# L1-distance attention of a fused vision tower: one score tile in sixteen moves from VectorE to ScalarE and TensorE

## The chip, the cores and the metric

The kernel runs on one core of a Trainium2 chip. The metric is the device time of one execution in microseconds (us), lower is better. The core has a matrix engine (TensorE, PE in the profile), a vector engine (VectorE, DVE), a scalar engine (ScalarE, ACT), a general engine (GpSimd, POOL) and a queue engine that issues most transfers (SyncE, SP). Each runs its own instruction list in order, and they meet at semaphores. SBUF is the working memory; PSUM, which TensorE writes, has eight banks of 512 f32 columns on 128 partitions, called `ps[0]` to `ps[7]` here.

## The reference

The program is a small vision tower: wavelet tokens, linear attention, a mixture of experts, an L1-distance attention, and a routed MLP, each on a layernorm of the stream `h` of 128 images, 64 tokens each, 64 wide. The change lies in the L1-distance attention, whose core is this:

```python
def one_query(qs):
    return -jnp.sum(jnp.abs(qs[:, None, :, :] - k), axis=-1) * scale
...
a = jnp.concatenate([a, jnp.zeros((b, 1, t, h), a.dtype)], axis=1)
a = jax.nn.softmax(a, axis=1)[:, :t]
bf = jnp.einsum('bsdh,bshw->bdhw', a, vf)
bb = jnp.einsum('bdsh,bshw->bdhw', a, vb)
o = (bf + bb).sum(axis=2).reshape(b, t, d)
y = o * jax.nn.sigmoid(1.702 * o)
y = y @ fanin_w.T + fanin_b
```

For every image, each of 64 x 64 pairs of tokens and each of 8 heads needs the sum of 64 absolute differences: 2,097,152 differences an image, or 16 tiles of 128 partitions x 1024.

## The kernel before

Images are worked on in 64 pairs (`pair`, one body in each engine's program; pairs 4 to 63 run in a hardware loop of two pairs a turn). Within a pair, image `b` = 0 comes first, then `b` = 1. In each image TensorE makes the 16 difference tiles in the order of the string `ORDER` (line 36, function `image`): position `k` in 0 to 15 is a letter. A tile is two f16 matmuls of 512 columns that pick a query row and subtract the keys (both sit as high and low f16 halves in `blocks`).

- **D tiles** (11 an image, line 760) alternate between banks 0/1 and 2/3. VectorE turns each into 16 columns of `score` by one reduction with absolute value over 128x1024 (`reduce`, line 1364). TensorE may write D tile d only when reduction d-2 is done.
- **A tiles** (5 an image, line 754) go one half each to banks 4 and 5. ScalarE takes the absolute value of each half into `absd0` or `absd1` (`absolute`, line 1004), and may be at most one tile behind. GpSimd sums the five tiles of an image in a tree of additions (`batch`, lines 1473 and 1477), and starts when all of them are there.

Between tiles, at written-out positions `k`, the function `extra` inside TensorE's `pair` hangs the rest of the attention:

```python
if k == 10:
    queries(q + 1, at)
if k == 12:
    low(q + 1, 1 - odd, 0)
if k == 14:
    keys(q + 1, 1 - odd)
```

`queries` (669) and `keys` (673) form the projections of the next pair in bank 6. ScalarE writes their high halves to `qk` as f16 (`high_q` 978, `high_k` 982). `low` then makes the same f32 product a second time (681 or 679) and subtracts the high half by one f16 matmul (682), and ScalarE stores what is left (986). SP copies `qk` into `blocks` (`fill_blocks`, 389). Other extras are `values_b` (689), `values_f` (696), the transpose of the inputs (`turn`, 663), the transposes of the attention (`turn_attn`, 704), its products with the values (`attend`, 720 and 725, in three parts), the transpose and projection of the gated result (`turn_y` 731, `fan_in` 735). Bank 7 is shared by `turn`, `attend`, `turn_y` and `fan_in`. When the scores of an image are done, SP spreads them into `attn` (`spread`, 8 transfers an image, 398). ScalarE takes eight exponentials of the previous pair, four after position 10 of image 1 and four after position 13 (`exponentials`, 1016). VectorE has three small steps a pair besides: `reciprocals` (1349), `finish` (1359) and `gated` (1354); GpSimd one, `normalise` (1484).

## Time and profile before

| | |
|---|---|
| runs, us | 2650.24, 2652.99, 2647.89 (median 2650.24) |
| profiled execution, us | 2650.77 |
| its span, us | 2648.9 |
| share of the span busy | PE 85%, DVE 85%, POOL 66%, ACT 56% |
| first score reduction to the end of the last | 717.7 to 2464.3 us |

The span is the time from the first to the last instruction that the profiler saw; the execution's own time is 1.9 us longer. Shares of busy time are means over all five stages, so they tell little of the attention stage alone. The attention stage is two thirds of the program and repeats one body, so one pair of images read in order of time stands for it. A matmul's row shows when it was issued and a modelled end; rows of PE therefore overlap, and the distance between two starts is the better measure of what one costs. An f32 matmul leaves two records.

### The profile page before, as it was taken

The page shows a single profiled execution, that of the slowest core. Times are in us where ns is not written, and L with a number is a line of the kernel's source. Part 1 is how long each engine was busy: PE and PEld are TensorE (multiplying, and loading weights), DVE is VectorE, ACT ScalarE, POOL GpSimd, SP SyncE. Part 2 cuts the span into 40 slices and gives each one's busy share as a digit, 9 for nine tenths or more (in the row PEclk, how much of TensorE's full clock was granted, in tenths as well). Part 3 has the DMA queues.
Part 4 walks back from the last instruction along what each step waited for, and adds up shares of the span by engine and source line. Part 5 has one row for each costly group of instructions (what it writes and reads, how often), then busy time and mean ns, then how long its engine had stood idle before and what let it go on. Part 6 is the DMA issues. An engine that isn't in the chain of part 4 may idle for free.

```text
span 2648.9 us, 45720 instructions
## 1 busy us (share of the span) xinstructions
PE 2259.4 (85%) x12251; PEld 971.9 (37%) x12251; DVE 2253.5 (85%) x2718; ACT 1474.8 (56%) x3767; POOL 1754.7 (66%) x1015
## 2 busy tenths in 40 slices
PE   5649999999388989899898989989898998989366
PEld 3433333333133333333333333333333333333255
DVE  2877778777699999999999999999999999999532
ACT  0325555555166666666666666666666666666234
POOL 0112333333188888889888888888888888888311
PEclk8879999999599999999999999999999999999678
DMA  5200000000022221222212122221212222121000
GB/s 130 61 0 1 1 0 0 0 0 0 19 50 51 50 50 45 51 50 51 50 47 52 46 50 50 50 50 47 52 46 50 50 51 50 47 52 46 13 12 20
DMA packets 163209, 101.97 MB, mean 38 GB/s; under 512 B 55773, under 2 KB 161182, under 8 KB 163039
## 3 DMA queue, kind: packets, MB, share of 16 engines
q1 hardware_dynamic: 162858, 101.41, 15.5%
q8 instruction: 18, 0.29, 0.1%
q10 hardware_dynamic: 316, 0.12, 0.0%
q14 instruction: 17, 0.14, 0.0%
HBM read 10.63 MB, written 4.19 MB: 6 GB/s over the span
## 4 chain that ended last, share of the span: by engine, by line
PE 62%; DVE 23%; issue 10%; DVEq 2%; ACT 1%; DMA 1%; POOL 1%; ACTq 0%; SPq 0%; POOLq 0%
DVE score L1364 17%; PE pp L760 16%; PE pp L754 7%; PE pp L594 5%; PE pp L725 3%; PE pp L615 2%; PE pp L681 2%; PE pp L673 2%; PE pp L619 2%; PE pp L689 2%; PE pp L669 2%; PE pp L679 2%; PE pp L616 2%; PE pp L620 2%; PE pp L586 2%
## 5 line engine op out<-in xcount | busy, mean ns | idle before, releaser
L1364 DVE TENSOR_REDUCE score<-pp 128x16 f32<-128x1024 f32 x1408 | 1647.1, 1219 | 103.2 <-PE pp L760 83.6
L1473 POOL TENSOR_TENSOR absd<-absd 128x2560 f32<-128x2560 f32 (+4 forms) x640 | 1453.8, 2272 | 199.8 <-ACT absd L1004 159.5
L760 PE MATMUL pp<-blocks,pick 128*128 128x512 f16 x2816 | 817.3, 383 | 154.9 <-DVE score L1364 150.5
L1004 ACT ACTIVATE absd<-pp 128x512 f32<-128x512 f32 x1280 | 695.5, 598 | 369.4 <-PE pp L754 365.5
L760 PEld LDWEIGHTS pp<-blocks,pick 128*128 128x128 f16 x2816 | 211.3, 98 | 590.6 <-DVE score L1364 421.3
L754 PE MATMUL pp<-blocks,pick 128*128 128x512 f16 x1280 | 400.3, 383 | 2.1
L1449 POOL TENSOR_TENSOR absd<-absd,yw 128x512 f32<-128x512 f32 x112 | 142.1, 1269 | 319.0 <-DVE yw L1286 319.0
L938 ACT ACTIVATE absd<-pp 128x512 f32<-128x512 f32 x256 | 150.8, 596 | 148.2 <-PE pp L616 146.9
L1302 DVE SCALAR_TENSOR_TENSOR absd<-pp,absd 128x512 f32<-128x512 f32 x256 | 172.6, 688 | 53.1 <-ACT absd L938 38.4
L754 PEld LDWEIGHTS pp<-blocks,pick 128*128 128x128 f16 x1280 | 119.9, 98 | 248.6 <-ACT absd L1004 84.2
L986 ACT CAST qk<-pp 128x512 f16<-128x512 f32 x130 | 76.0, 585 | 191.2 <-PE pp L682 191.2
L1016 ACT ACTIVATE expd<-attn 128x65 f32<-128x65 f32 x512 | 157.4, 329 | 0.0
L594 PE MATMUL pp<-absd 128*64 128x512 f32 x512 | 138.1, 618 | 0.0
L1016 ACT ACTIVATION_READ_ACCUMULATOR expd<-attn 128x1 f32 x512 | 107.7, 210 | 0.0
L615 PE MATMUL pp<-x,absd 128*128 128x512 f16 x256 | 98.4, 384 | 0.6 <-issue 0.2
L619 PE MATMUL pp<-x,absd 128*128 128x512 f16 x256 | 97.8, 382 | 0.3
L620 PE MATMUL pp<-x,absd 128*128 128x512 f16 x256 | 97.5, 381 | 0.0
L616 PE MATMUL pp<-x,absd 128*128 128x512 f16 x256 | 97.5, 381 | 0.0
L1510 POOL COPY xs<-xn 128x256 f32 x16 | 8.0, 528 | 127.7 <-PEq L855 93.0
L1286 DVE TENSOR_TENSOR yw<-pp,absd 128x512 f32<-128x512 f32 x112 | 77.2, 689 | 17.8 <-PE pp L594 15.3
L725 PEld LDWEIGHTS pp<-vb,attk 64*64 64x64 f32 x2048 | 71.0, 137 | 52.9 <-issue 52.6
L942 ACT COPY absd<-pp 128x512 f32<-128x512 f32 x128 | 74.9, 585 | 27.8 <-PE pp L586 18.9
(209 smaller groups left out, 2578.7 us busy)
## 6 DMA issues: line engine op xcount, KB each, us to landing
blocks<-qk SPq DMA_DIRECT2D x1032, 64.0 KB, 2.0
attn<-score SPq DMA_DIRECT2D x1024, 16.0 KB, 1.8
xs<-xn SPq DMA_DIRECT2D x66, 32.0 KB, 1.8
big<-in_wrb_t SPq DMA_DIRECT2D x1, 2064.0 KB
big<-in_x_rows SPq DMA_DIRECT2D x4, 512.0 KB, 6.4
token_rows<-big SPq DMA_DIRECT2D x8, 256.0 KB, 2.0
big<-in_L_ffn_w SPq DMA_DIRECT2D x4, 512.0 KB, 9.8
out<-big SPq DMA_DIRECT2D x16, 128.0 KB, 2.0
```

What stands on the lines that cost most here:

```text
L594: mm = pe.matmul(ps[4 + k % 2][64 * e:64 * e + 64, :], w3[:, 2 * k + e, :], hid[:, 2 * (k % 2) + e, :], start=True, stop=True)
L615: pe.matmul(ps[e], w12_hi[:, 0, 2 * k + e, :], x2[:, b, :], start=True, stop=False)
L616: pe.matmul(ps[e], w12_lo[:, 0, 2 * k + e, :], x2[:, b, :], start=False, stop=True).then_inc(C["h1_ps"], 1)
L619: pe.matmul(ps[2 + e], w12_hi[:, 1, 2 * k + e, :], x2[:, b, :], start=True, stop=False)
L754: pe.matmul(ps[4 + n], pick[:, unit % 8, :], blocks[:, b, unit // 16, unit // 8 % 2, :], start=True, stop=True).then_inc(X["diffA"], 1)
L760: mm = pe.matmul(ps[bank + n], pick[:, unit % 8 + n, :], blocks[:, b, unit // 16, unit // 8 % 2, :], start=True, stop=True)
L938: nc.scalar.activation(silu[:, e, :], ps[e], ACT.Silu, scale=1.0 / W_SCALE).then_inc(C["silu"], 1)
L1004: nc.scalar.activation(absd[odd][:, 16 * u + 8 * n:16 * u + 8 * n + 8, :], ps[4 + n].rearrange("p (h w) -> p h w", w=D), ACT.Abs).then_inc ...
L1016: op = nc.scalar.activation(expd[:, n, :], attn[:, :, n], ACT.Exp, scale=-(float(D) ** -0.5), accum_out=zst[:, 0, n:n + 1])
L1302: dve.scalar_tensor_tensor(out=hid[:, 2 * (k % 2) + e, :], in0=ps[2 + e], scalar=1.0 / W_SCALE, in1=silu[:, e, :], op0=ALU.mult, op1=ALU.m ...
L1364: dve.tensor_reduce(score[:, odd, b, 16 * d:16 * d + 16], pp[:, bank:bank + 2, :].rearrange("p n (h w) -> p (n h) w", w=D), AX.X, ALU.add, ...
L1473: nc.gpsimd.tensor_tensor(x[:, :, 0:w], x[:, :, 0:w], x[:, :, w:2 * w], ALU.add).then_inc(X["tree"], 1)
```

## The change

- `ORDER` becomes `DADDADDADDADADED`: 10 D tiles, 5 A tiles, and one new **E tile** at position 14 of each image.
- The E tile is made with its operands swapped: keys and queries of the tile lie on the partitions (`blocks` is the stationary operand, four matmuls of 256 columns into banks 4 and 5). ScalarE takes its absolute values into `abse`, the last quarter of `absd0` and `absd1` (line 1060 of the changed kernel).
- TensorE sums it over partitions (`sum_e`, 759): four f32 matmuls, each with the 128 x 32 matrix `pair_ones` as stationary operand and 256 moving columns, into the four quarters of 32 partitions of bank 7. ScalarE copies 256 columns to `esum` (`copy_e`, 1067), TensorE turns them by two f32 matmuls with 8 moving columns (`turn_e`, 765), and ScalarE copies 16 columns to `score` (`take_e`, 1074), which raises the new semaphore `etaken`. SP's `spread` waits for it besides.
- In `low` the repeated f32 product is gone: the f16 matmul accumulates onto the product that `queries` or `keys` left in bank 6.
- The eight exponentials come in four parts of two.
- `gated` moves from after D tile 8 to after D tile 7 of image 1; `turn_attn` from position 4 to 5. GpSimd's work is the same five tiles. `c_cols` shares memory with `absd0`, a constant `c_row` is loaded to `row_of` by one more transfer, and `pair_ones` is set by five memsets at the start of the program; of these the constant's values, its declaration and `c_cols` are left out below.

```diff
-ORDER = "DADDADDADDADDADD"
-ND, NA = ORDER.count("D"), ORDER.count("A")
+ORDER = "DADDADDADDADADED"
+ND, NP = ORDER.count("D"), ORDER.count("A")
+NA = NP + 1
 W_SCALE = 64.0
...
         neg_eye = sb("neg_eye", [P, P], F16)
+        pair_ones = sb("pair_ones", [P, 32])
+        row_of = sb("row_of", [P, HEADS])
+        esum = sb("esum", [P, 2 * P])
         xs1 = sb("xs1", [P, 2 * D])
...
         tok_rows = big[:].rearrange("p (u n) -> p u n", u=8)
-        absd = [t[:].rearrange("p (n w) -> p n w", w=D) for t in (absd0, absd1)]
+        absd = [t[:, 0:NP * 1024].rearrange("p (n w) -> p n w", w=D) for t in (absd0, absd1)]
+        abse = [t[:, NP * 1024:NA * 1024].rearrange("p (m n) -> p m n", m=4) for t in (absd0, absd1)]
         wk_b = big[0:D, 0:QK].rearrange("p (h d) -> p h d", d=D)
...
             sp.dma_start(rank[:], a["c_rank"]).then_inc(moe_in, 16)
+            sp.dma_start(row_of[:], a["c_row"]).then_inc(l1_in, 16)
             sp.dma_start(both[:].rearrange("p a b -> p (a b)"), a["c_both"]).then_inc(moe_in, 16)
...
                 sp.wait_ge(X["pooled"], 2 * p + b + 1)
+                sp.wait_ge(X["etaken"], 2 * p + b + 1)
                 if not first:
...
                     pe.wait_ge(X["sum"], p - 3)
+                if 1 <= at < 3:
+                    pe.wait_ge(X["etaken"], 2 * p - 3)
                 pe.wait_ge(X["xs"], 16 * (p + 1))
...
                 pe.wait_ge(X["half"], 4 * p + 2 * kind + 1)
-                if kind:
-                    pe.matmul(ps[6], xT1[:, odd, :], wk_diag[:].rearrange("p h d -> p (h d)"), start=True, stop=False)
-                else:
-                    pe.matmul(ps[6], xTq[:], wqv[:, 0:QK], start=True, stop=False)
-                pe.matmul(ps[6], neg_eye[:], qk[:, kind, 0, :], start=False, stop=True).then_inc(X["klo_ps" if kind else "qlo_ps"], 1)
+                pe.matmul(ps[6], neg_eye[:], qk[:, kind, 0, :], start=False, stop=True, skip_group_check=True).then_inc(X["klo_ps" if kind else "qlo_ps"], 1)
             def values_b(p, odd, at):
...
                 if part == 0:
+                    pe.wait_ge(X["etaken"], 2 * p + 5)
                     pe.wait_ge(X["attq"], p + 1)
...
                 pe.matmul(ps[7][:, 192:256], yT[:], fan[:], start=True, stop=True).then_inc(X["fan_ps"], 1)
+            def sum_e(s, b, first):
+                pe.wait_ge(X["abs"], 2 * NA * s + 2 * NA)
+                if not first:
+                    pe.wait_ge(X["etaken"], s)
+                for m in range(4):
+                    mm = pe.matmul(ps[7][32 * m:32 * m + 32, 0:2 * P], pair_ones[:], abse[b][:, m, :], start=True, stop=True)
+                mm.then_inc(X["e_ps"], 1)
+            def turn_e(s):
+                pe.wait_ge(X["esum"], s + 1)
+                for g in range(2):
+                    mm = pe.matmul(ps[7][:, 256 + 8 * g:264 + 8 * g], esum[:, P * g:P * g + P], row_of[:], start=True, stop=True)
+                mm.then_inc(X["et_ps"], 1)
             def image(q, b, at, extra):
...
                             pe.wait_ge(X["red"], ND * s + d - 1)
-                        unit, bank, done = 2 * d, 2 * ((b + d) % 2), "diffD"
+                        unit, bank, done = 2 * d, 2 * (d % 2), "diffD"
                         d += 1
...
                                 pe.wait_ge(X["abs"], 2 * NA * s + 2 * u + n - 1)
-                            unit = 2 * (ND + u) + n
-                            pe.matmul(ps[4 + n], pick[:, unit % 8, :], blocks[:, b, unit // 16, unit // 8 % 2, :],
-                                      start=True, stop=True).then_inc(X["diffA"], 1)
+                            if path == "A":
+                                unit = 2 * (ND + u) + n
+                                mm = pe.matmul(ps[4 + n], pick[:, unit % 8, :], blocks[:, b, unit // 16, unit // 8 % 2, :],
+                                               start=True, stop=True)
+                            else:
+                                for m in range(2):
+                                    mm = pe.matmul(ps[4 + n][:, 256 * m:256 * m + 256],
+                                                   blocks[:, b, 1, 1, P * (2 * n + m):P * (2 * n + m) + P],
+                                                   pick[:, 6:8, :].rearrange("p a b -> p (a b)"), start=True, stop=True)
+                            mm.then_inc(X["diffA"], 1)
                         u += 1
...
                             queries(q + 1, at)
+                        if k == 11 and at >= 1:
+                            sum_e(2 * q - 1, 1, False)
+                        if k == 13 and at >= 1:
+                            turn_e(2 * q - 1)
                         if k == 12:
...
                             low(q + 1, 1 - odd, 1)
+                        if k == 2:
+                            sum_e(2 * q, 0, at == 0)
+                        if k == 4:
+                            turn_e(2 * q)
                         if at >= 2:
-                            if k == 4:
+                            if k == 5:
                                 turn_attn(q - 2)
...
             fan_in(last - 2)
+            pe.wait_ge(X["sum"], last - 1)
+            sum_e(2 * last + 1, 1, False)
+            turn_e(2 * last + 1)
+            pe.wait_ge(X["etaken"], 2 * PAIRS)
             for p, odd in ((last - 1, 0), (last, 1)):
...
                         act.wait_ge(X["pooled"], s - 1)
-                    nc.scalar.activation(absd[odd][:, 16 * u + 8 * n:16 * u + 8 * n + 8, :],
-                                         ps[4 + n].rearrange("p (h w) -> p h w", w=D), ACT.Abs).then_inc(X["abs"], 1)
+                    if u == NP and n == 0 and not first:
+                        act.wait_ge(X["e_ps"], s - 1)
+                    if u < NP:
+                        nc.scalar.activation(absd[odd][:, 16 * u + 8 * n:16 * u + 8 * n + 8, :],
+                                             ps[4 + n].rearrange("p (h w) -> p h w", w=D), ACT.Abs).then_inc(X["abs"], 1)
+                    else:
+                        nc.scalar.activation(abse[odd][:, 2 * n:2 * n + 2, :].rearrange("p m n -> p (m n)"), ps[4 + n],
+                                             ACT.Abs).then_inc(X["abs"], 1)
+            def copy_e(s):
+                act.wait_ge(X["e_ps"], s + 1)
+                act.wait_ge(X["et_ps"], s)
+                nc.scalar.copy(esum[:], ps[7][:, 0:2 * P]).then_inc(X["esum"], 1)
+            def take_e(s, p, odd, b, at):
+                act.wait_ge(X["et_ps"], s + 1)
+                if at >= 2:
+                    act.wait_ge(X[f"spread{b}"], 16 * 8 * (p - 1))
+                nc.scalar.copy(score[:, odd, b, 240:256], ps[7][:, 256:272]).then_inc(X["etaken"], 1)
             def exponentials(p, part, first):
...
                         act.wait_ge(X["zr"], p)
-                for n in range(4 * part, 4 * part + 4):
+                for n in range(2 * part, 2 * part + 2):
                     op = nc.scalar.activation(expd[:, n, :], attn[:, :, n], ACT.Exp, scale=-(float(D) ** -0.5),
                                               accum_out=zst[:, 0, n:n + 1])
-                if part:
+                if part == 3:
                     op.then_inc(X["exp"], 1)
...
                 high_q(q + 1, False)
+                if at >= 1:
+                    copy_e(s - 1)
+                absolute(s, 0, 4, first)
                 low(q + 1, 0)
-                absolute(s, 0, 4, first)
+                if at >= 1:
+                    take_e(s - 1, q - 1, 1 - odd, 1, at - 1)
+                absolute(s, 0, 5, first)
                 s += 1
...
                 absolute(s, 1, 0, first)
+                copy_e(s - 1)
                 absolute(s, 1, 1, first)
+                take_e(s - 1, q, odd, 0, at)
                 if at >= 2:
...
                 absolute(s, 1, 2, first)
+                if at >= 1:
+                    exponentials(q - 1, 0, at == 1)
                 absolute(s, 1, 3, first)
...
                 if at >= 1:
-                    exponentials(q - 1, 0, at == 1)
+                    exponentials(q - 1, 1, at == 1)
                 absolute(s, 1, 4, first)
                 if at >= 1:
-                    exponentials(q - 1, 1, at == 1)
+                    exponentials(q - 1, 2, at == 1)
+                absolute(s, 1, 5, first)
+                if at >= 1:
+                    exponentials(q - 1, 3, at == 1)
             act.wait_ge(pads, PADS)
...
             values_f(last, 1)
+            copy_e(2 * last + 1)
+            take_e(2 * last + 1, last, 1, 1, 4)
             for p in (last - 1, last):
...
                 if p < last:
-                    exponentials(last, 0, False)
-                    exponentials(last, 1, False)
+                    for part in range(4):
+                        exponentials(last, part, False)
             layernorm_act(act, 3)
...
                 dve.memset(t, 1.0).then_inc(pads, 1)
+            for half in range(2):
+                at = slice(64 * half, 64 * half + 64)
+                dve.memset(pair_ones[at, half:half + 1], 1.0)
+                dve.memset(pair_ones[at, 1 - half:2 - half], 0.0)
+            dve.memset(pair_ones[:, 2:32], 0.0)
             dve.memset(wk_bd[:], 0.0)
...
                 dve.wait_ge(X["diffD"], ND * s + d + 1)
-                bank = 2 * ((b + d) % 2)
+                bank = 2 * (d % 2)
                 dve.tensor_reduce(score[:, odd, b, 16 * d:16 * d + 16],
...
                             finish(q - 3, slot)
-                        if b == 1 and d == 8 and at >= 2:
+                        if b == 1 and d == 7 and at >= 2:
                             gated(q - 2)
...
                 x = absd[b]
-                pool.wait_ge(X["abs"], 2 * NA * (s + 1))
+                pool.wait_ge(X["abs"], 2 * NA * s + 2 * NP)
                 for m, w in enumerate((32, 16, 8, 4, 2)):
...
                     pool.wait_ge(X[f"spread{b}"], 16 * 8 * (p - 1))
-                nc.gpsimd.tensor_tensor(score[:, odd, b, 16 * ND:256].unsqueeze(2), x[:, :, 0:1], x[:, :, 1:2],
+                nc.gpsimd.tensor_tensor(score[:, odd, b, 16 * ND:16 * ND + 16 * NP].unsqueeze(2), x[:, :, 0:1], x[:, :, 1:2],
                                         ALU.add).then_inc(X["pooled"], 1)
```

On TensorE, image 0 of one pair from position 7 to position 14, before. L754 is an A tile, L760 a D tile (`x4` is two of them), L669 `queries`, L681/L682 and L679/L682 `low`, L673 `keys`:

```order
L754 MATMUL pp<-blocks,pick 128x512 x2
L760 MATMUL pp<-blocks,pick 128x512 x2
L663 MATMUL pp<-ident,xs 128x128
L760 MATMUL pp<-blocks,pick 128x512 x2
L754 MATMUL pp<-blocks,pick 128x512 x2
L669 MATMUL pp<-wqv,xTq 128x512
L760 MATMUL pp<-blocks,pick 128x512 x4
L681 MATMUL pp<-wqv,xTq 128x512
L682 MATMUL pp<-qk,neg_eye 128x512
L754 MATMUL pp<-blocks,pick 128x512 x2
L760 MATMUL pp<-blocks,pick 128x512 x2
L673 MATMUL pp<-wk_diag,xT 128x512
```

The changed kernel, from `queries` at position 10 to position 1 of image 1. L786 is an A tile, L798 a D tile, L790 the E tile, L686 `queries`, L759 `sum_e` of the image before, L695 `low`, L765 `turn_e`, L690 `keys`:

```order
L686 MATMUL pp<-wqv,xTq 128x512
L798 MATMUL pp<-blocks,pick 128x512 x2
L759 MATMUL pp<-absd,pair_ones 32x256 x4
L786 MATMUL pp<-blocks,pick 128x512 x2
L695 MATMUL pp<-qk,neg_eye 128x512
L798 MATMUL pp<-blocks,pick 128x512 x2
L765 MATMUL pp<-row_of,esum 128x8 x2
L790 MATMUL pp<-pick,blocks 128x256 x4
L690 MATMUL pp<-wk_diag,xT 128x512
L798 MATMUL pp<-blocks,pick 128x512 x4
L695 MATMUL pp<-qk,neg_eye 128x512
L786 MATMUL pp<-blocks,pick 128x512 x2
```

Between `queries` and the D tile of position 15 there were three D tiles and one A tile; now there are two D tiles, an A tile, the E tile, `sum_e` and `turn_e`, while the second product (L681, and L679 behind it) is gone.

On ScalarE, image 1 of one pair in the changed kernel, from its second A tile on. L1057 is the absolute value of an A tile's halves, L1060 of the E tile's, L1074 `take_e`, L1092 the copy of the turned attention, L1096 the tanh of `gated`, L1085 the exponentials:

```order
L1057 ACTIVATE absd<-pp 128x512 x2
L1074 COPY score<-pp 128x16
L1092 COPY attq<-pp 128x512
L1057 ACTIVATE absd<-pp 128x512 x2
L1085 ACTIVATE expd,zst<-attn 128x65 x2
L1057 ACTIVATE absd<-pp 128x512 x2
L1096 ACTIVATE osb<-pp 128x64
L1085 ACTIVATE expd,zst<-attn 128x65 x2
L1057 ACTIVATE absd<-pp 128x512 x2
L1085 ACTIVATE expd,zst<-attn 128x65 x2
L1060 ACTIVATE absd<-pp 128x512 x2
L1085 ACTIVATE expd,zst<-attn 128x65 x2
```

Before, four exponentials stood behind the tile of position 10 and four behind that of position 13, the last tile of the image on ScalarE; now two stand behind each of positions 7, 10, 12 and 14.

## Rows read from the trace of the kernel before

**Rows 1.** Windows: us busy of PE, PEld, DVE, ACT, POOL; granted clock, DMA share, GB/s.

```profile
2200.00:2400.00 200.00, 181.50 (x1030) 74.05 (x1029) 190.87 (x184) 127.40 (x348) 179.27 (x96) 1.00 0.20 49
```

**Rows 2.** Waits of the whole span: total us, times, longest us.

```profile
PEld pp L760 <- DVE score L1364: 421.3, 713, 1.1
...
DVE score L1364 <- PE pp L760: 83.6, 254, 17.0
```

**Rows 3.** Groups of instructions: busy us, mean ns of one, idle before.

```profile
L1364 DVE TENSOR_REDUCE score<-pp 128x16 f32<-128x1024 f32 x1408 | 1647.1, 1219 | 103.2 <-PE pp L760 83.6
...
L527 PE MATMUL pp<-absd 128*128 128x64 f32 x128 | 15.8, 276 | 1.5 <-ACT absd L905 1.1
```

**Rows 4.** GpSimd's timeline: start us, duration us, line, operation, count, idle before.

```profile
1411.00 11.75 POOL L1473 TENSOR_TENSOR absd<-absd 128x2560 f32<-128x2560 f32 x5 [0.91 <-ACT absd L1004]
...
1424.24 11.68 POOL L1473 TENSOR_TENSOR absd<-absd 128x2560 f32<-128x2560 f32 x5 [1.01 <-ACT absd L1004]
...
1438.19 11.69 POOL L1473 TENSOR_TENSOR absd<-absd 128x2560 f32<-128x2560 f32 x5 [0.78 <-ACT absd L1004]
```

**Rows 5.** VectorE's timeline over one pair.

```profile
1400.06 0.20 DVE L1349 RECIPROCAL zst<-zst 128x8 f32<-128x8 f32 x1
1400.42 3.49 DVE L1364 TENSOR_REDUCE score<-pp 128x16 f32<-128x1024 f32 x3 [0.16 <-PE pp L760]
...
1403.97 3.49 DVE L1364 TENSOR_REDUCE score<-pp 128x16 f32<-128x1024 f32 x3
1407.62 2.36 DVE L1364 TENSOR_REDUCE score<-pp 128x16 f32<-128x1024 f32 x2 [0.16 <-PE pp L760]
1410.21 10.88 DVE L1364 TENSOR_REDUCE score<-pp 128x16 f32<-128x1024 f32 x9 [0.24 <-PE pp L760]
1421.45 2.36 DVE L1364 TENSOR_REDUCE score<-pp 128x16 f32<-128x1024 f32 x2 [0.36 <-PE pp L760]
```

**Rows 6.** TensorE's timeline over the same pair.

```profile
1402.31 1.08 PE L696 MATMUL pp<-wqv,xT 96*64 96x256 f32 x8
1403.32 0.60 PE L760 MATMUL pp<-blocks,pick 128*128 128x512 f16 x2
...
1405.25 0.61 PE L760 MATMUL pp<-blocks,pick 128*128 128x512 f16 x2 [0.35 <-DVE score L1364]
...
1406.12 1.02 PE L669 MATMUL pp<-wqv,xTq 96*128 96x512 f32 x2
1406.98 1.13 PE L760 MATMUL pp<-blocks,pick 128*128 128x512 f16 x4
1407.97 1.12 PE L681 MATMUL pp<-wqv,xTq 96*128 96x512 f32 x2
1408.93 0.38 PE L682 MATMUL pp<-qk,neg_eye 128*128 128x512 f16 x1
1409.15 0.59 PE L754 MATMUL pp<-blocks,pick 128*128 128x512 f16 x2
...
1417.45 0.69 PE L720 MATMUL pp<-vf,attq 128*64 128x64 f32 x16
1418.07 0.60 PE L760 MATMUL pp<-blocks,pick 128*128 128x512 f16 x2
```

**Rows 7.** ScalarE's timeline over the same pair.

```profile
1405.15 0.25 ACT L967 COPY xT<-pp 64x128 f32<-64x128 f32 x1
...
1421.87 0.33 ACT L1016 ACTIVATE expd<-attn 128x65 f32<-128x65 f32 x1
...
1423.09 1.08 ACT L1004 ACTIVATE absd<-pp 128x512 f32<-128x512 f32 x2
1424.04 0.34 ACT L1016 ACTIVATE expd<-attn 128x65 f32<-128x65 f32 x1
```

**Rows 8.** SP's queue over the same pair.

```profile
1414.32 5.30 SPq L389 DMA_DIRECT2D blocks<-qk  x8
```

**Rows 9.** The page: transfers, count, KB each, median us from issue to landing.

```profile
attn<-score SPq DMA_DIRECT2D x1024, 16.0 KB, 1.8
```

More of the change, by code:

```diff
@@ L96, in constants @@
         both[1, e, e // 2, e % 2] = 1.0 / LO_SCALE
+    row_of = np.zeros((4, 32, 4, 2))
+    for m in range(4):
+        for a in range(2):
+            row_of[m, a, m, a] = 1.0
     same_head = np.kron(np.eye(16), np.ones((8, 8)))
@@ L103, in constants @@
         "c_both": both.reshape(64, 8 * P).astype(np.float16),
+        "c_row": row_of.reshape(P, HEADS).astype(np.float32),
         "c_head": same_head.astype(np.float32),
@@ L129, in build @@
         c_rows = sb("c_rows_sb", [P, 64])
-        c_cols = sb("c_cols_sb", [7, 2, 8, P])
         tok_w = sb("tok_w", [7, D])
@@ L146, in build @@
         absd0 = sb("absd0", [P, NA * 1024])
+        c_cols = absd0[0:7, 0:2048].rearrange("p (o c m) -> p o c m", o=2, c=8)
         kT = absd0[:, 2048:3072].rearrange("p (b a m) -> p b a m", b=2, a=4)
@@ L266, in build @@
             "xs", "wk_in", "consts", "xT_ps", "xT_sb", "xTq", "q_ps", "k_ps", "qlo_ps", "klo_ps", "half", "tb0", "tb1",
-            "diffD", "diffA", "red", "abs", "tree", "pooled", "spread0", "spread1", "exp", "zr", "attk", "attq_ps", "attq",
+            "diffD", "diffA", "red", "abs", "tree", "pooled", "e_ps", "esum", "et_ps", "etaken", "spread0", "spread1", "exp", "zr", "attk", "attq_ps", "attq",
             "o_ps", "tanh", "y", "yT_ps", "yT", "fan_ps", "hx", "sum", "vb_ps", "vb", "vf_ps", "vf")}
@@ L313, in build @@
         MOE_IN = 16 * 6
-        L1_IN = 16 * 5
+        L1_IN = 16 * 6
         GATE = 14
@@ L735, in fan_in @@
                 pe.matmul(ps[7][:, 192:256], yT[:], fan[:], start=True, stop=True).then_inc(X["fan_ps"], 1)
+            def sum_e(s, b, first):
+                pe.wait_ge(X["abs"], 2 * NA * s + 2 * NA)
+                if not first:
+                    pe.wait_ge(X["etaken"], s)
+                for m in range(4):
+                    mm = pe.matmul(ps[7][32 * m:32 * m + 32, 0:2 * P], pair_ones[:], abse[b][:, m, :], start=True, stop=True)
[5 more added lines that the diff above has]
+                mm.then_inc(X["et_ps"], 1)
             def image(q, b, at, extra):
@@ L858, in _ @@
         def _(act):
-            act.dma_start(c_cols[:].rearrange("p a b c -> p (a b c)"), a["c_cols"]).then_inc(tok_in, 16)
+            act.dma_start(c_cols.rearrange("p a b c -> p (a b c)"), a["c_cols"]).then_inc(tok_in, 16)
             act.dma_start(tok_w[:], a["L0_tok_W"]).then_inc(tok_in, 16)
```

## Prediction

> **What bounds the kernel now.** I read first how busy the engines are in a stretch of the attention stage: in 200 us at full clock (1.00) VectorE is busy 190.9, TensorE 181.5, GpSimd 179.3 and ScalarE 127.4 [rows 1]. Three engines lie within 7% of each other, so no single one can be relieved and leave the rest as it was. Next the waits: TensorE's tile matmuls and their weight loads wait for VectorE's reductions 421.3 us in total; VectorE waits for TensorE's tiles 83.6 us [rows 2]. So VectorE sets the pace and TensorE, now and then, makes it late. Then one pair of images in order of time. From tree sum to tree sum of the same image GpSimd takes 1438.19 - 1411.00 = 27.19 us [rows 4]; that is the period of a pair. There are 1408 reductions [rows 3], 22 a pair, so 64 pairs.
>
> *VectorE's period.* Three reductions back to back take 3.49 us and the last of them 1.22 (the group's mean) [rows 3, 5], so one follows another after (3.49 - 1.22)/2 = 1.135 us. 22 of them are 24.97. The reciprocal costs 1400.42 - 1400.06 = 0.36, `finish`, which stands between two groups, 1403.97 - (1400.42 + 3 x 1.135) = 0.15 [rows 5], and I give `gated` 0.13: 0.64 in all. 25.61 of 27.19 us are work; 1.58 us a pair are stalls. They show as 0.24 and 0.36 of idle time ahead of groups, and inside the run of nine reductions, which takes 10.88 us where 8 x 1.135 + 1.22 is 10.30 [rows 5].
>
> *GpSimd's period.* It is idle 1.01 and 0.78 us ahead of two tree sums of a pair [rows 4], so its own work is 27.19 - 1.79 = 25.40 us. The change leaves that work alone. **25.40 is a floor** for the new period.
>
> **How a stall comes about.** A reduction that waits for its tile starts 0.64 us after the tile's first matmul (1406.98 on TensorE, 1407.62 on VectorE). It lasts 1.22, and TensorE issues the next tile but one 0.06 later (the reduction of 1403.97 ends at 1405.19, the D tile that waited for it starts at 1405.25) [rows 5, 6]. Two reductions take 2.27, so TensorE has 2.27 - 0.64 - 1.28 = **0.35 us of slack**. I count with one rule: from one D tile to the next TensorE's lateness grows by (its work - 1.135), and never falls below zero; what is over 0.35 is a stall of VectorE.
>
> TensorE's pieces, as distances between starts [rows 6]: a tile 0.43 (1405.25 to 1406.12 is two); an f32 product of 512 columns 0.86 (1406.12 to 1406.98); `low` 1409.15 - 1407.97 = 1.18, of which the f16 part 0.22; `values_f` 1.01 (1402.31 to 1403.32); a part of `attend` 0.62. By this rule the old order gives 1.76 us of stalls, the trace 1.58: I scale what the rule gives by 0.9.
>
> **The change, part by part.**
>
> 1. *A D tile less an image.* VectorE loses 2 x 1.135 = 2.27 us a pair. 20 reductions and 0.64 are 23.34 us. VectorE falls below GpSimd's floor.
>
> 2. *The repeated product goes.* TensorE loses 2 x 0.96 (1.18 less 0.22) = 1.92 us a pair, in image 0 right where the extras are densest.
>
> 3. *The E tile.* Four f16 matmuls of 256 columns stream as many columns as two of 512, so 0.43 us; if their weight loads don't hide it is at most twice that. I take 0.43. ScalarE's two halves cost 0.95 us (1423.09 to 1424.04) [rows 7], 1.9 a pair.
>
> 4. *`sum_e`.* No row shows a matmul whose stationary operand has 32 columns. Nearest is `values_f`, four f32 matmuls of 256 columns by 64 stationary ones. By the product of 512 columns each streams 0.43, so one after another they would take 1.72, and they take 1.01: two run side by side, with 0.15 over. Four side by side would take 0.43 + 0.15 = 0.58; one after another 1.72 + 0.15 = 1.87. I take 0.7, near the lower end because the nearest row shows the overlap; both ends are kept. The Trainium skill, TensorEngine Tiling (Array Packing), Theoretical Speedup, says up to four times for 32 columns or fewer; by it `sum_e` costs 0.58 by the trace's durations and the period falls another 0.1. The same page under Key Properties speaks against the change: a switch of the tiling mode drains the engine, and there are four more of these a pair. The 0.15 over in `values_f` is what the trace shows of that.
>
> 5. *`turn_e`.* 64 f32 matmuls with 128 stationary and 64 moving columns keep TensorE busy 15.8 us [rows 3], 0.25 each; two of them 0.5. Bounds: 0.3 and 0.7.
>    With 4 and 5, TensorE gains 2 x 1.2 and loses 1.92: its load grows by 0.5 us a pair, and over 20 reductions instead of 22.
>
> 6. *The walk.* TensorE's work up to each D tile, where the slack is used up:
>    - image 0, position 6: `values_f` behind `fan_in`, 0.04 of stall.
>    - position 11: tile, `queries`, tile = 1.72, stall 0.23 (the lateness stays at 0.35).
>    - position 13: 0.7 + 0.43 + 0.22 + 0.43 = 1.78, stall 0.65.
>    - position 15: 0.5 + 0.43 + 0.86 + 0.43 = 2.22, and 0.2 for `keys`, which waits until ScalarE has taken the low half; stall 1.28.
>    - image 1, positions 8 to 11, with `attend`: 1.48, 1.04, 1.47, stall 0.24. `sum_e` and `turn_e` of that image (positions 2 and 4) stay in the slack, since the repeated product is gone from position 0.
>    - positions 12 to 15: here it is ScalarE. Two exponentials cost half of 1423.09 - 1421.87, 0.61. From the tile of 10 to that of 12 ScalarE needs 0.95 + 0.1 (my estimate for the tanh of 64 columns) + 0.61 = 1.66, then 1.56 to the E tile; VectorE wants a D tile each 1.135. TensorE's E tile needs both banks free, so D tile 15 is some 0.6 us past its slack. Stall 0.62. Before, there were two D tiles between the last two tiles of ScalarE.
>
>    Sum 3.06, scaled 2.7 us. Period 23.34 + 2.7 = 26.1 us (rounded up), 0.7 above GpSimd's floor.
>
> 7. *ScalarE's copies.* `copy_e` of 256 columns lies between 0.25 (64x128) and 0.6 (128x512) [rows 7], `take_e` at 0.2 or less. They're covered: ScalarE's load grows by some 2.6 us a pair to about 19 of 26. Without that cover they would add to the wait at position 15, already counted.
>
> 8. *The new wait on SP.* `spread` of image 1 now waits for `take_e`, about 1.5 us later than the tree sum that it waited for. Behind it queue eight transfers of `spread` and eight of `fill_blocks` for the next pair, 5.30 us for each eight [rows 8], and 1.8 us of landing [rows 9]: 12.4 us after `take_e`. In the walk above the next pair's first D tile comes 13.8 us after `take_e`. The exponentials need the spread, landed after 5.3 + 1.8 = 7.1 us, and come 7.9 us after. Cost: nothing, with 0.8 to 1.4 us to spare; should both miss, it is a case of the hand-offs below.
>
> 9. *Once only.* Memsets, the constant, the last `sum_e`: beside other work or under 2 us. Nothing.
>
> Sum: (27.19 - 26.1) x 64 = 70 us, less about 1 for the tail. The profiled execution took 2650.77 us, as good as the median (2650.24). **Predicted: 2582 us.**
>
> **Rivals.**
>
> - *GpSimd's floor* (chance 0.18). The bursts overlap with waits that I count singly, or `sum_e` runs at 0.58 and ScalarE catches up; then the tree sums go gapless at 25.4 to 25.8. For it: only 0.7 us lie between. Against it: bursts of over 2 us at position 15 are larger than any before. 2650.8 - 1.79 x 64 = 2536 to 2562.
> - *The hand-offs cost more* (0.20). `sum_e`, copy, turn, copy are four steps between TensorE and ScalarE in each image, in an order where either engine may be busy for 1 us. Half a microsecond more at each `turn_e` of image 0 and at ScalarE's end of image 1 gives 26.5 to 27.0: 2607 to 2639. If `sum_e` runs two at a time (1.01) this is also where it lands, 26.5.
> - *Slower: TensorE becomes the bound* (0.11). The 32-column matmuls run one after another, 1.87 us each time. Position 13 then stalls 1.2 more, image 1 needs 0.43 + 1.87 before its position 3 and stalls 0.8 and 0.2; times 0.9 is 2.0 more, 28.1 us, +58: 2709. At 1.3 us for `sum_e` 27.1 comes out by the same steps; from about 1.35 on the kernel is slower. Against it: `values_f` overlaps.
> - *No effect* (0.06), 27.14 to 27.24: the exact cancellation of the one against the other; I see no mechanism that puts it there. That `start=False` would make the product again is excluded by the list of instructions.
>
> The forecast itself, 25.8 to 26.5, has 0.45: 2562 to 2607. A difference of 0.2% (5.3 us) is about what a measurement of this kernel can tell. Faster: 0.45 + 0.18 + 0.20 = 0.83. The range goes from the floor, 2537, to the end of the hand-off case, 2640; what it leaves out is the slower case, no effect, and edges.
>
> **What would show it.** Right: 1280 reductions; the period of the tree sums 26.1 and GpSimd idle about 0.7 a pair; VectorE's idle time largest ahead of the reductions of image 0's positions 13 and 15; four `sum_e` matmuls start within 0.7 us of the next tile; the second product's rows gone. Wrong: GpSimd without gaps (floor), `sum_e` over 1.3 us from start to next start, ScalarE's absolute values never waiting for TensorE in image 1 (then ScalarE is the bound), or SP's `spread` late enough that the exponentials or the first tile of a pair wait for a transfer.

## The result, and the profile after

| | before | after |
|---|---|---|
| median, us | 2649.56 (4 runs) | 2584.01 (2582.76 to 2585.15, 4 runs) |
| ratio | | 0.9748, 95% interval 0.9733 to 0.9762 |
| span of the profiled execution, us | 2648.9 | 2581.7 |
| period of a pair, us (tree sum to tree sum, one pair) | 27.19 | 26.24 |
| the same as the median over all pairs, us | 27.19 | 26.28 |
| start of the first score reduction to start of the last, us | 717.7 to 2463.1 | 717.5 to 2396.9 |

The change makes the kernel 65.5 us faster; the prediction said 2582. The whole gain lies in the attention stage, which is 65.8 us shorter from its first reduction to the start of the last. The median over all pairs is taken between the starts of two pairs' first reductions. A window of that stage in the changed kernel (us busy of PE, PEld, DVE, ACT, POOL; granted clock, DMA share, GB/s), to be read against [rows 1]:

```profile
2000.00:2200.00 200.00, 189.38 (x1222) 84.36 (x1223) 179.34 (x176) 155.34 (x432) 184.65 (x101) 1.00 0.24 51
```

VectorE, the busiest before with 190.9, is now the third with 179.3. TensorE has gone from 181.5 to 189.4, GpSimd from 179.3 to 184.7, ScalarE from 127.4 to 155.3. The waits of the whole span (us, times, longest), to be read against [rows 2]:

```profile
PEld pp L798 <- DVE score L1452: 232.4, 523, 1.0
...
DVE score L1452 <- PE pp L798: 181.1, 320, 13.2
```

TensorE's weight loads wait little more than half as long for VectorE (421.3 to 232.4), and VectorE waits twice as long for TensorE (83.6 to 181.1): who is late has changed. GpSimd's timeline, the answer to [rows 4] (start, duration, line, operation, count, idle before):

```profile
1410.08 11.67 POOL L1561 TENSOR_TENSOR absd<-absd 128x2560 f32<-128x2560 f32 x5
...
1423.24 11.72 POOL L1561 TENSOR_TENSOR absd<-absd 128x2560 f32<-128x2560 f32 x5 [1.01 <-ACT absd L1057]
...
1435.32 1.04 POOL L1572 TENSOR_TENSOR attk<-expd,zst 128x512 f32<-128x512 f32 x1
1436.32 11.65 POOL L1561 TENSOR_TENSOR absd<-absd 128x2560 f32<-128x2560 f32 x5
```

The period is 1436.32 - 1410.08 = 26.24 us. Behind `normalise` (1435.32) the next tree sum starts without any wait; only the sum of image 1's tiles waits, 1.01 us for ScalarE. VectorE's timeline over the same pair, the answer to [rows 5]:

```profile
1407.31 1.23 DVE L1452 TENSOR_REDUCE score<-pp 128x16 f32<-128x1024 f32 x1 [0.16 <-PE pp L798]
1409.06 1.23 DVE L1452 TENSOR_REDUCE score<-pp 128x16 f32<-128x1024 f32 x1 [0.53 <-PE pp L798]
1411.41 9.28 DVE L1452 TENSOR_REDUCE score<-pp 128x16 f32<-128x1024 f32 x8 [1.12 <-PE pp L798]
1421.04 1.23 DVE L1452 TENSOR_REDUCE score<-pp 128x16 f32<-128x1024 f32 x1 [0.36 <-PE pp L798]
...
1422.39 1.23 DVE L1452 TENSOR_REDUCE score<-pp 128x16 f32<-128x1024 f32 x1
1424.08 2.36 DVE L1452 TENSOR_REDUCE score<-pp 128x16 f32<-128x1024 f32 x2 [0.46 <-PE pp L798]
1426.35 0.19 DVE L1437 RECIPROCAL zst<-zst 128x8 f32<-128x8 f32 x1
1426.46 3.44 DVE L1452 TENSOR_REDUCE score<-pp 128x16 f32<-128x1024 f32 x3
```

Each idle time is a late tile. In image 0: position 11 0.16 us, position 13 0.53, position 15 1.12. In image 1: position 11 0.36, position 15 0.46. TensorE's timeline over the two dense stretches, the answer to [rows 6]:

```profile
1406.67 0.60 PE L798 MATMUL pp<-blocks,pick 128*128 128x512 f16 x2
1407.20 0.64 PE L759 MATMUL pp<-absd,pair_ones 128*32 128x256 f32 x8
1407.77 0.60 PE L786 MATMUL pp<-blocks,pick 128*128 128x512 f16 x2
...
1408.86 0.51 PE L765 MATMUL pp<-row_of,esum 128*128 128x8 f32 x4
1409.22 0.60 PE L790 MATMUL pp<-pick,blocks 128*128 128x256 f16 x4
1409.81 1.12 PE L690 MATMUL pp<-wk_diag,xT 96*128 96x512 f32 x2
1410.78 1.03 PE L798 MATMUL pp<-blocks,pick 128*128 128x512 f16 x4
...
1421.76 0.59 PE L798 MATMUL pp<-blocks,pick 128*128 128x512 f16 x2
1422.73 0.88 PE L790 MATMUL pp<-pick,blocks 128*128 128x256 f16 x4 [0.38 <-ACT absd L1057]
1423.45 1.03 PE L798 MATMUL pp<-blocks,pick 128*128 128x512 f16 x4
```

`sum_e` (L759) takes 1407.77 - 1407.20 = 0.57 us from start to next start, `turn_e` (L765) 0.36, the E tile (L790) with what stands before `keys` (L690) 0.59: 0.43 for the tile itself, as in `e2_tile_only` below, where `keys` starts that long after it, and 0.16 of waiting. At 1422.73 the E tile of image 1 waited 0.38 us for ScalarE, and its four matmuls took 0.72 instead of 0.43, since the second half had to wait for the second bank, which ScalarE's row of 1422.08 below reads until 1423.17. ScalarE's timeline shows why, the answer to [rows 7]:

```profile
1420.39 1.09 ACT L1057 ACTIVATE absd<-pp 128x512 f32<-128x512 f32 x2 [1.77 <-PE pp L786]
...
1422.08 1.09 ACT L1057 ACTIVATE absd<-pp 128x512 f32<-128x512 f32 x2
1423.03 0.34 ACT L1085 ACTIVATE expd<-attn 128x65 f32<-128x65 f32 x1
...
1423.63 1.10 ACT L1060 ACTIVATE absd<-pp 128x512 f32<-128x512 f32 x2
```

From the absolute values of position 10 (1420.39) to those of 12 (1422.08) ScalarE needs 1.69 us, and from there to those of the E tile (1423.63) 1.55. VectorE takes a D tile each 1.135.

### The profile page after: what moved, and what is told of

Its sections match the earlier page's. It is cut to its first block, busy times and chain, and to the rows that moved or that the text cites. A ratio compares the mean times of both kernels' runs of the same rounds, so it can differ in the third digit from the quotient of the medians.

```text
span 2581.7 us, 50257 instructions
## 1 busy us (share of the span) xinstructions
PE 2269.1 (88%) x13783; PEld 1036.1 (40%) x13783; DVE 2105.3 (82%) x2595; ACT 1661.8 (64%) x4279; POOL 1753.1 (68%) x1015
## 4 chain that ended last, share of the span: by engine, by line
PE 59%; DVE 21%; issue 9%; ACT 7%; DVEq 2%; DMA 1%; ACTq 0%; POOL 0%; SPq 0%; POOLq 0%
DVE score L1452 14%; PE pp L798 14%; PE pp L786 5%; PE pp L609 5%; ACT absd L1057 4%; PE pp L740 3%; PE pp L690 3%; PE pp L759 3%; PE pp L630 2%; PE pp L634 2%; PE pp L686 2%; PE pp L635 2%; PE pp L631 2%; PE pp L790 2%; PE pp L765 2%
## 5 line engine op out<-in xcount | busy, mean ns | idle before, releaser
L1452 DVE TENSOR_REDUCE score<-pp 128x16 f32<-128x1024 f32 x1280 | 1499.0, 1217 | 182.5 <-PE pp L798 181.1
L1057 ACT ACTIVATE absd<-pp 128x512 f32<-128x512 f32 x1280 | 695.5, 597 | 225.3 <-PE pp L786 225.1
L798 PE MATMUL pp<-blocks,pick 128*128 128x512 f16 x2560 | 749.1, 382 | 56.0 <-DVE score L1452 48.6
L786 PE MATMUL pp<-blocks,pick 128*128 128x512 f16 x1280 | 394.7, 382 | 9.3 <-ACT absd L1057 0.5
L798 PEld LDWEIGHTS pp<-blocks,pick 128*128 128x128 f16 x2560 | 202.5, 100 | 386.9 <-DVE score L1452 232.4
L988 ACT ACTIVATE absd<-pp 128x512 f32<-128x512 f32 x256 | 150.8, 596 | 148.0 <-PE pp L631 143.4
L786 PEld LDWEIGHTS pp<-blocks,pick 128*128 128x128 f16 x1280 | 114.6, 97 | 206.8 <-ACT absd L1057 59.7
L1085 ACT ACTIVATE expd<-attn 128x65 f32<-128x65 f32 x512 | 163.1, 337 | 0.0
L1060 ACT ACTIVATE absd<-pp 128x512 f32<-128x512 f32 x256 | 143.1, 632 | 0.0
L790 PE MATMUL pp<-pick,blocks 128*128 128x256 f16 x512 | 88.6, 274 | 29.9 <-ACT absd L1057 23.8
L1085 ACT ACTIVATION_READ_ACCUMULATOR expd<-attn 128x1 f32 x512 | 111.4, 218 | 0.0
```

What stands on the lines that cost most here:

```text
L786: mm = pe.matmul(ps[4 + n], pick[:, unit % 8, :], blocks[:, b, unit // 16, unit // 8 % 2, :], start=True, stop=True)
L798: mm = pe.matmul(ps[bank + n], pick[:, unit % 8 + n, :], blocks[:, b, unit // 16, unit // 8 % 2, :], start=True, stop=True)
L988: nc.scalar.activation(silu[:, e, :], ps[e], ACT.Silu, scale=1.0 / W_SCALE).then_inc(C["silu"], 1)
L1057: nc.scalar.activation(absd[odd][:, 16 * u + 8 * n:16 * u + 8 * n + 8, :], ps[4 + n].rearrange("p (h w) -> p h w", w=D), ACT.Abs).then_inc ...
L1085: op = nc.scalar.activation(expd[:, n, :], attn[:, :, n], ACT.Exp, scale=-(float(D) ** -0.5), accum_out=zst[:, 0, n:n + 1])
L1452: dve.tensor_reduce(score[:, odd, b, 16 * d:16 * d + 16], pp[:, bank:bank + 2, :].rearrange("p n (h w) -> p (n h) w", w=D), AX.X, ALU.add, ...
```

## The experiments

All ran beside the kernel before; its medians there were 2651.5 to 2652.4 us, 2 to 3 us above its 2649.56 beside the changed kernel. The changed kernel was not run again with them, so a difference to its 2584.01 us is uncertain by as much; the periods of a pair, medians over all pairs of the profiled execution, say the same thing without that. *Bursts theory*: a stall arises where TensorE's work between two D tiles runs out of its 0.35 us of slack. *Relief theory*: what counts is how much work VectorE has, or any engine in total.

**The two halves alone: `e1_product_only` and `e2_tile_only`.** The first is the kernel before with this edit of `low` and nothing else, the second the changed kernel with it undone:

```diff
-                if kind:
-                    pe.matmul(ps[6], xT1[:, odd, :], wk_diag[:].rearrange("p h d -> p (h d)"), start=True, stop=False)
-                else:
-                    pe.matmul(ps[6], xTq[:], wqv[:, 0:QK], start=True, stop=False)
-                pe.matmul(ps[6], neg_eye[:], qk[:, kind, 0, :], start=False, stop=True).then_inc(...)
+                pe.matmul(ps[6], neg_eye[:], qk[:, kind, 0, :], start=False, stop=True, skip_group_check=True).then_inc(...)
```

> The kernel before, with only the repeated f32 product of low taken out: 16 tiles as before, no E tile. Bursts theory (a stall comes where TensorE's work between two D tiles exceeds 1.135 us by more than 0.35 us of slack): positions 14 and 15 of image 0 and position 2 of image 1 lose 0.96 us each of what stalled VectorE or lies ahead of it; the walk leaves 0.5 us of stalls a pair, period 25.61 + 0.5 = 26.1 us, 2580 us in all, as fast as the full change; the E tile then adds nothing to it. Relief theory (the gain is VectorE's, whose load falls by 2.27 us a pair): VectorE's load is unchanged here, so most of the gain is gone: 2630 to 2645 us.

> The changed kernel with the repeated f32 product put back into low: E tile, sums and split exponentials, but TensorE has 1.92 us a pair more. Bursts theory: 0.96 more at position 13 of image 0, 0.5 more at positions 2 and 3 of image 1: period 27.6 us, 2670 us, slower than before. Relief theory: VectorE is still relieved by 2.27 us a pair, so 2590 to 2620 us.

Measured: product alone 2594.52 us (2587.64 to 2605.66; ratio 0.9773, 0.9752 to 0.9793); tile alone 2650.77 (0.9993, 0.9984 to 1.0003). Without the E tile most of the gain is there (58 of some 66 us); with the product left in, the E tile and all that comes with it are worth nothing. The relief theory is out: it had 2630 to 2645 for the first and 2590 to 2620 for the second. In `e2_tile_only` VectorE has 2.27 us less to do a pair, and its timeline shows where most of them go:

```profile
1412.05 1.22 DVE L1456 TENSOR_REDUCE score<-pp 128x16 f32<-128x1024 f32 x1 [1.39 <-PE pp L802]
1414.14 7.15 DVE L1456 TENSOR_REDUCE score<-pp 128x16 f32<-128x1024 f32 x6 [0.87 <-PE pp L802]
```

They go into idle time ahead of positions 13 and 15 of image 0: 1.39 and 0.87 us, where the change has 0.53 and 1.12; and the period is 27.33. The bursts theory comes nearer and still misses: it said 2670, slower than before, 0.3 us a pair too much, and the kernel is no slower. Its 0.96 more at position 13 are there (0.86), but position 15 got cheaper by 0.25: with the product in the way TensorE reaches the E tile later, and from there to the tile behind `keys` it takes 1.29 us (1412.22 to 1413.51) where the change takes 1.56 (1409.22 to 1410.78), since `keys` no longer waits. `e1_product_only` was to be at 2580. Its period is 26.38 where the walk had 26.1, which is 18 us too much for a miss of 14; the rest is TensorE's clock, the subject of the last two runs, which costs this kernel some 5 us and the kernel before 9.

**The exponentials: `e3_exp_clear` and `e4_exp_old`.** Both are the changed kernel with the parts of the exponentials placed otherwise:

```diff
 e3_exp_clear, ScalarE, image 1 (e4_exp_old: parts 0 and 1 behind position 10, 2 and 3 behind 12)
                 absolute(s, 1, 2, first)
                 if at >= 1:
                     exponentials(q - 1, 0, at == 1)
+                    exponentials(q - 1, 1, at == 1)
                 absolute(s, 1, 3, first)
                 if at >= 2:
                     gate_o(q - 2)
-                if at >= 1:
-                    exponentials(q - 1, 1, at == 1)
                 absolute(s, 1, 4, first)
-                if at >= 1:
-                    exponentials(q - 1, 2, at == 1)
                 absolute(s, 1, 5, first)
                 if at >= 1:
+                    exponentials(q - 1, 2, at == 1)
                     exponentials(q - 1, 3, at == 1)
```

> The changed kernel with the eight exponentials in two fours, behind positions 7 and 14 of image 1, so that nothing stands between ScalarE's absolute values of positions 10, 12 and 14 but the tanh. Bursts theory: VectorE's idle 0.36 and 0.46 us at the end of image 1 go to under 0.2 together; period 25.6 us, 2543 us. Rival (ScalarE's stretch is hidden, its total load counts): unchanged, 2584 us.

> The changed kernel with the exponentials where they stood before, four behind position 10 and four behind the next A tile (12). Bursts theory: ScalarE needs 0.6 us more between 10 and 12 and 0.6 more between 12 and 14, all of it on the path: period 27.2 to 27.4 us, 2645 to 2660 us: without the four parts the change would gain nothing. Rival (hidden): 2584 us.

Measured: 2569.56 us (0.9686, 0.967 to 0.9702) and 2620.66 (0.9883, 0.9866 to 0.9899). ScalarE's stretch is on the path, in both directions: 14 us are gained by clearing it (period 26.04 for 26.28), 37 lost by the old placement (26.87). With the old placement the E tile would make the kernel 26 us slower than `e1_product_only`; the four parts are what lets it be no loss. But each placement moved less than I said (2543, and 2645 to 2660). VectorE's timeline of `e3_exp_clear` at the end of image 1:

```profile
1417.86 3.49 DVE L1450 TENSOR_REDUCE score<-pp 128x16 f32<-128x1024 f32 x3
1421.26 0.19 DVE L1435 RECIPROCAL zst<-zst 128x8 f32<-128x8 f32 x1
1421.62 3.48 DVE L1450 TENSOR_REDUCE score<-pp 128x16 f32<-128x1024 f32 x3 [0.17 <-PE pp L798]
```

The 0.46 us of idle time are gone (three reductions run through from 1417.86), but the step over the reciprocal takes 0.36 us again, with 0.17 of waiting for TensorE, where the changed kernel has 1426.46 - 1426.35 = 0.11: VectorE, now earlier, meets `values_b` and the next A tile, the burst behind it. The 0.36 us ahead of position 11, which were to shrink too, are unchanged. In `e4_exp_old` only the second of the two intervals costs (the wait before position 15 grows from 0.46 to 1.06 us):

```profile
1411.29 2.35 DVE L1450 TENSOR_REDUCE score<-pp 128x16 f32<-128x1024 f32 x2 [1.06 <-PE pp L798]
```

**Where a load lies: `e5_sum_twice_0` and `e6_sum_twice_1`.** The four matmuls of `sum_e` are issued twice, in the first for the set that stands in image 0, in the second for that in image 1; the second set overwrites the first with the same sums.

```diff
-                for m in range(4):
+                for m in [n for _ in range(2 if b == 1 else 1) for n in range(4)]:
```

> The changed kernel with the four sum matmuls that stand at position 11 of image 0 done twice. Bursts theory: they stand in the densest stretch, where TensorE is past its slack, so all of the second set is paid, 0.45 to 0.55 us a pair: 2612 to 2619 us. Rival (TensorE's total load counts, wherever it lies): the same time as the run with the other image's sums doubled.

> The changed kernel with the four sum matmuls that stand at position 2 of image 1 done twice. Bursts theory: TensorE waits for VectorE 0.24 us right before them, and the run of eight reductions around them has hardly a gap; most of the second set goes into the slack: 0 to 0.2 us a pair, 2584 to 2597 us. Rival (total load): as the run with image 0's doubled.

Measured: 2610.99 us (0.9851, 0.9834 to 0.9867) and 2602.68 (0.9819, 0.9802 to 0.9835). The second set costs TensorE 0.44 us (two sets 1.01, one 0.57). In image 0 that comes to 27 us or 0.42 a pair, nearly all of it, a microsecond under the range; in image 1 to 18.7 us or 0.29, 6 us over its range. The two kernels' runs don't overlap (2608.79 to 2613.16, 2601.85 to 2604.34). The place matters, as the theory says, though by 8 us and not by 15 or more, for image 1 had less slack than I gave it: the set also makes the later `turn_attn` late, and a wait of 0.16 us appears in its run of reductions.

**Another order: `e7_keys_later` and `e8_product_keys`.** `keys` moves out of the densest stretch, with ScalarE's `low` behind the first absolute value of image 1. `e7_keys_later` does this to `e3_exp_clear`, `e8_product_keys` to `e1_product_only`:

```diff
-                        if k == 14:
-                            keys(q + 1, 1 - odd)
...
                         if k == 0:
+                            keys(q + 1, 1 - odd)
+                        if k == 2:
                             low(q + 1, 1 - odd, 1)
...
                 high_k(q + 1)
-                low(q + 1, 1)
                 absolute(s, 1, 0, first)
+                low(q + 1, 1)
```

> The changed kernel with the exponentials of e3_exp_clear and with keys moved from position 14 of image 0 to position 0 of image 1, the low half behind it from position 0 to position 2. Bursts theory: the stall of 1.12 us at position 15 shrinks to some 0.3, a stall of 0.2 appears at position 2; period 25.3 to 25.5 us, where GpSimd's tree sums are gapless and take over as the bound: 2530 to 2542 us. Rival (the transfers of the next pair's keys, now 1 to 2 us later, hold up its first tile): 2560 to 2580 us.

> The kernel before with the repeated product taken out and keys moved in the same way, no E tile and the exponentials where they were. Bursts theory: its stalls were small already, VectorE is at 25.61 us a pair and little is to be had: period 25.8 to 26.0 us, 2565 to 2585 us with the dips of TensorE's clock as in e1_product_only. If it comes within 5 us of e7_keys_later, the E tile is worth nothing in any order; if it is 30 us above, the E tile pays once the bursts are spread.

Measured: 2536.92 us (0.9571, 0.9555 to 0.9587) and 2608.57 (0.9839, 0.9822 to 0.9855). `e7_keys_later` beats both kernels, 47 us below the changed one: 14 by the exponentials of `e3_exp_clear`, 33 by `keys`. VectorE's timeline there:

```profile
1413.10 1.23 DVE L1449 TENSOR_REDUCE score<-pp 128x16 f32<-128x1024 f32 x1 [0.16 <-PE pp L798]
1414.86 8.62 DVE L1449 TENSOR_REDUCE score<-pp 128x16 f32<-128x1024 f32 x7 [0.53 <-PE pp L798]
1423.64 2.37 DVE L1449 TENSOR_REDUCE score<-pp 128x16 f32<-128x1024 f32 x2 [0.16 <-PE pp L798]
1426.37 1.23 DVE L1449 TENSOR_REDUCE score<-pp 128x16 f32<-128x1024 f32 x1 [0.35 <-PE pp L798]
```

The stall of 1.12 us at position 15 is gone. GpSimd's timeline says what is next: its sums wait 0.26 to 0.38 us a pair.

```profile
1402.40 11.67 POOL L1558 TENSOR_TENSOR absd<-absd 128x2560 f32<-128x2560 f32 x5 [0.26 <-ACT absd L1056]
...
1415.43 11.67 POOL L1558 TENSOR_TENSOR absd<-absd 128x2560 f32<-128x2560 f32 x5
...
1427.98 11.72 POOL L1558 TENSOR_TENSOR absd<-absd 128x2560 f32<-128x2560 f32 x5 [0.38 <-ACT absd L1056]
```

The rival (late transfers) is out. The same move without the E tile missed my expectation by 24 us and is slower than `e1_product_only`: that kernel had no stall at position 15 to remove, and VectorE's timeline shows a new one, ahead of position 2 of image 1:

```profile
1418.84 5.75 DVE L1360 TENSOR_REDUCE score<-pp 128x16 f32<-128x1024 f32 x5 [0.16 <-PE pp L756]
1424.75 5.86 DVE L1360 TENSOR_REDUCE score<-pp 128x16 f32<-128x1024 f32 x5 [0.16 <-PE pp L756]
```

1424.75 is 0.24 us later than five reductions of 1.135 behind 1418.84. The prediction's rule gives this: `keys` and two tiles are 1.72 us, 0.23 over 1.135 and the slack. I had not applied it to this kernel. So the E tile pays once the bursts are spread: 2537 with it, 2589 (below) at best without it among the orders tried. That isn't a clean price of the tile, as no run has the exponentials of `e3_exp_clear` and no E tile.

**TensorE's clock: `e9_product_fill` and `e10_before_fill`.** The runs of `e1_product_only` scatter over 18 us (2587.64, 2590.77, 2598.27 and 2605.66, with mean granted clocks of 0.954, 0.954, 0.950 and 0.947), and its TensorE shows matmuls at half speed now and then. Windows of 4 us of the kernel before (columns as above):

```profile
1284.00:1288.00 4.00, 2.42 (x10) 0.52 (x8) 4.00 (x5) 3.76 (x20) 2.68 (x4) 0.95 0.00 0
1288.00:1292.00 4.00, 4.00 (x12) 1.70 (x11) 2.23 (x4) 1.20 (x3) 4.00 (x1) 0.63 0.40 99
1292.00:1296.00 4.00, 3.95 (x22) 1.57 (x20) 4.00 (x5) 2.69 (x7) 3.84 (x3) 1.00 0.21 53
```

TensorE is busy 2.42 of 4 us while VectorE catches up at the end of image 1; right behind it the granted clock is 0.63 of full as the mean of 4 us: the 1.2 GHz level for some 3 us, and then 2.4 again. TensorE's timeline at that place:

```profile
1287.53 1.02 PE L760 MATMUL pp<-blocks,pick 128*128 128x512 f16 x2 [0.66 <-DVE score L1364]
1288.35 1.91 PE L689 MATMUL pp<-wqv,xT 96*128 96x512 f32 x2
1290.06 1.06 PE L754 MATMUL pp<-blocks,pick 128*128 128x512 f16 x2
```

The f32 product (L689) lasts 1.91 us there and 1.02 at full clock. In the stage the kernel before has five such dips, all at this place of a pair, behind waits of 0.40, 0.53 and 0.66 us; `e1_product_only` has eight in its profiled execution (the slowest of its runs, 2605.66) and `e8_product_keys` two, all at the same place; the changed kernel and the other runs with an E tile have none. But the quiet stretch is there in every pair: one pair earlier (1256.70 to 1260.70) TensorE is busy 2.42 of 4 us just so, and the granted clock stays at 1.00. The five dips come 382 us apart, 14 periods. Two kernels give TensorE something to do that nobody waits for:

```diff
+                            if k >= 13:
+                                pe.matmul(ps[6], neg_eye[:], pick[:, 0:4, :].rearrange("p a b -> p (a b)"), start=True, stop=True)
```

> e1_product_only with one f16 matmul of 512 columns of constants into the idle bank 6 behind each of positions 13, 14 and 15 of image 1, where TensorE waits 0.4 to 0.66 us for VectorE; nobody reads the result. It adds 0.64 us of work a pair to TensorE that nothing waits for. Clock theory (TensorE's clock dips of some 3 us cost time because TensorE is less busy in this kernel than in the changed one, which has none): the dips between 760 and 2400 us become fewer than the eight of e1_product_only or vanish, time 2580 to 2588 us and a narrower spread of runs. Rival (dips come at random or by power, busy TensorE doesn't help): eight dips or more, 2590 us or above.

> The kernel before with the same three matmuls of constants a pair behind positions 13 to 15 of image 1. Clock theory: its five dips vanish, each cost some 1.6 us: 2641 to 2646 us, 5 to 10 us faster than before though it does more. Rival: same time or slower, 2650 to 2655 us.

Measured: 2589.10 us (2588.03 to 2589.83; 0.9765, 0.9752 to 0.9778) and 2642.86 (2642.06 to 2644.45; 0.997, 0.9957 to 0.9982). No dip is left in the stage in either. The kernel before becomes 8.9 us faster by doing more, with its median period unchanged at 27.19. For the product alone the scatter shrinks from 18 us to 2, and the period stays 26.38; the time is 1 us above the expected 2580 to 2588.

## Why the prediction was right

- *Which engine* (a D tile less; a burst of TensorE sets the time). Right. VectorE's waits for TensorE doubled, at the positions that the walk named.
- *The pieces.* `sum_e` 0.57 us, where I took 0.7 between 0.58 and 1.87: a second set in `e5_sum_twice_0` adds 0.44, what one such product streams alone (0.43), so the four matmuls of 32 stationary columns run side by side. The Trainium skill, TensorEngine Tiling (Array Packing), Theoretical Speedup, says up to four times for this, and the trace agrees. The drain of a mode switch, which its Key Properties name, can be at most the other 0.13; no run here shows it by itself. `turn_e` 0.36, where I took 0.5. The E tile 0.43, as taken.
- *The stalls.* A stall costs what the distance between two starts has over 1.135 us; the idle time shown is 0.09 less, since back to back a reduction of 1.22 us overlaps the next. By the rule, before its scaling by 0.9, and by the distances: position 11 of image 0 0.23 and 0.25; position 13 0.65 and 0.62; position 15 1.28 and 1.22; ScalarE at the end of image 1 0.62 and 0.56. Only image 1, positions 8 to 11, is off: 0.24 and 0.55 (1421.04 - 1411.41 - 8 x 1.135). Position 6, 0.04, shows no stall.
- *Two errors of the sum, one against the other.* These stalls are 3.2 us together, where the scaled sum had 2.7. The factor 0.9 was a misreading. The 0.36 us that I booked for the reciprocal hold a wait of 0.16 for a tile, printed in the row of 1400.42 in [rows 5]; where nothing waits, the step costs 0.11 (1426.46 - 1426.35). So the three small steps were priced at 0.64 us, and in the changed kernel cost some 0.46, of it 0.22 for `gated`; and the stalls before were about 1.85 us and not 1.58 (27.19 less 24.97 and some 0.37 of steps), close to the 1.76 of the rule, which needed no scaling. The scaled stalls are too small and the steps too dear.
- *The period.* 26.1 predicted, 26.28 as the median over all pairs. (27.19 - 26.28) x 64 = 58 us.
- *What I didn't see.* The other 8 us are the clock: the kernel before has five dips and the changed one none, and the run with fill, whose period is that of the kernel before, puts their price at 8.9 us. The error of the period, 0.18 x 64 = 12 us, and the dips nearly cancel. That the predicted time is within 2 us of the measured one is in good part luck, and the two errors above help the period; the places of the stalls and most of their sizes are not luck.
- *What I didn't say.* I summed the parts and did not ask what each is worth alone. The removed product carries the gain; the E tile with the split exponentials adds about 10 us to it. Once the clock is held some 5 are left (2589.10 against 2584.01), which the ratios alone don't separate from nothing (0.9752 to 0.9778 against 0.9733 to 0.9762); the periods, 26.38 and 26.28, say 6.
- *The cover.* SP's new wait cost nothing, as said. GpSimd's floor was not reached: it waits 1.01 us a pair, where I said 0.7, and its own work is 26.24 - 1.01 = 25.23, where I said 25.40.
- *Rivals.* Serial `sum_e`: out (0.57). GpSimd's floor: out here, almost reached in `e7_keys_later`. Costlier hand-offs: out, as the period is under their 26.5.

Left open: why image 1 loses 0.55 us ahead of position 11, in the kernel before as in the changed one, and has so little slack in `e6_sum_twice_1` (0.15 of the 0.44 us were hidden); and why only every fourteenth pair of the kernel before has a dip, though every pair has the quiet stretch. No run tried stretches of other lengths.

## What to carry to other kernels

Where two engines hand tiles over through two buffers, count the producer's work between two tiles, not its total: within one pair TensorE waited 0.40, 0.53 and 0.66 us for VectorE at the end of image 1 and was itself late with its tiles in image 0. Before moving work to a third engine, try to move or drop what makes the producer late: here dropping the repeated product gave 58 us, and the offload some 10 on top of it; with the exponentials in their old place it cost 26. Look at the idle time printed in a row before its distance is booked as work. Test the parts of a compound change alone, as the sum hides which one works.

## What the hardware showed that I had not expected

TensorE's granted clock fell to its lower level for some 3 us, again and again, in a kernel whose TensorE is 91% busy in the stage, each time at the place of the pair where it had waited 0.40, 0.53 and 0.66 us in turn, but in five of 64 pairs only. It cost 8.9 us of 2650, and three matmuls a pair whose result nobody reads took it away. It also accounts for the 8 us by which the change gained more than its period says. Runs of one kernel that scatter by 18 us can have this cause: the granted clock has to be read in stretches of a few us, as the mean over 200 us shows 0.99 or 1.00.
